# Differential attention with a routed FFN: the sum of the two scaled softmaxes as an accumulating transfer

## The reference

```python
A1 = einsum('bhqd,bhkd->bhqk', Q1, K1) * s        # Q and K have two halves of 64 each
A2 = einsum('bhqd,bhkd->bhqk', Q2, K2) * s
P = softmax(A1) - lam * softmax(A2)
O = einsum('bhqk,bhkd->bhqd', P, V)
Y = concat_heads(O) @ Wo + bo                      # then a layer norm over 128, times 0.2
```

## Time and profile before

| what | us |
|---|---|
| median of 3 runs (1209.81 to 1214.95) | 1213.73 |
| the profiled execution's own time | 1207.97 |
| its span | 1206.2 |
| TensorE busy | 1168.2 (97%) |
| GpSimd busy | 1017.3 (84%) |
| ScalarE busy | 968.9 (80%) |
| VectorE busy | 905.6 (75%) |
| the additions on GpSimd, 256 in all | 609.0 |
| the scalings on GpSimd, 256 in all | 307.1 |

### The profile page before, as it was taken

How to read it: one execution, slowest core, us unless ns; L and a number is a source line. 1 busy time by engine, 2 the same in 40 slices (tenths; PEclk the granted TensorE clock), 3 DMA queues, 4 the chain that set the end, 5 groups by cost and what they waited for, 6 DMA issues and landing times.

```text
span 1206.2 us, 28081 instructions
## 1 busy us (share of the span) xinstructions
PE 1168.2 (97%) x9730; PEld 841.2 (70%) x9730; DVE 905.6 (75%) x1573; ACT 968.9 (80%) x1711; POOL 1017.3 (84%) x657
## 2 busy tenths in 40 slices
PE   5899999999999999999999999999999999998998
PEld 4666767666677776767676767676767776765797
DVE  8878878786787878887878887877887877874510
ACT  3398888887888888988888988888888888985432
POOL 3599999999999999999999999999999999989000
PEclk8999999999999999999999999999999999997999
DMA  8832211221112111222221112221112221110000
GB/s 208 312 80 51 50 44 49 49 49 42 23 39 49 49 49 44 49 49 49 49 49 40 30 34 49 49 49 43 49 49 49 49 49 42 25 28 1 1 18 18
DMA packets 74134, 63.41 MB, mean 53 GB/s; under 512 B 45172, under 2 KB 63092, under 8 KB 74100
## 3 DMA queue, kind: packets, MB, share of 16 engines
q1 hardware_dynamic: 73092, 62.78, 20.3%
q10 hardware_dynamic: 880, 0.19, 0.1%
q0 software_dynamic: 128, 0.01, 0.0%
HBM read 19.96 MB, written 9.44 MB: 24 GB/s over the span
## 4 chain that ended last, share of the span: by engine, by line
PE 75%; POOL 19%; DVE 4%; issue 1%; ACT 0%; DMA 0%; DVEq 0%; SPq 0%; POOLq 0%; ACTq 0%
PE ps L517 24%; PE ps L533 18%; PE ps L547 16%; POOL p_mix L431 11%; PE ps L472 7%; POOL work L428 5%; PE ps L559 4%; PE ps L611 3%; PE ps L598 2%; PE ps L499 1%; DVE pt L862 1%; DVE small L906 1%; POOL wqk_lo L343 1%; POOL w L406 0%; POOL wqk_hi L340 0%
## 5 line engine op out<-in xcount | busy, mean ns | idle before, releaser
L906 DVE TENSOR_REDUCE small<-ps 128x1 f32<-128x1024 f32 x512 | 613.8, 1220 | 114.6 <-PE ps L517 113.9
L431 POOL TENSOR_TENSOR p_mix<-p_mix,work 128x1024 f32<-128x1024 f32 x256 | 609.0, 2379 | 21.4
L533 PEld LDWEIGHTS ps<-ident,p_mix 64*128 64x128 f32 x4096 | 309.6, 139 | 191.7 <-issue 168.1
L725 ACT ACTIVATE pt<-ps 128x512 f32<-128x512 f32 x512 | 305.6, 597 | 131.2 <-PE ps L533 120.7
L533 PE MATMUL ps<-ident,p_mix 64*128 64x64 f32 x4096 | 352.6, 226 | 15.7 <-POOL p_mix L431 11.2
L428 POOL TENSOR_SCALAR work<-work,small 128x1024 f32<-128x1024 f32 x256 | 307.1, 1200 | 42.8 <-DVE small L931 42.8
L712 ACT ACTIVATE p_mix<-ps,small 128x1024 f32<-128x1024 f32 x256 | 284.8, 1113 | 15.4 <-DVE small L906 15.3
L712 ACT ACTIVATE work<-ps,small 128x1024 f32<-128x1024 f32 x256 | 284.4, 1111 | 12.5 <-DVE small L906 12.5
L547 PE MATMUL ps<-pt,v_h 128*64 128x512 f32 x1024 | 248.7, 606 | 0.0
L517 PE MATMUL ps<-k_hi,q_hi 64*128 64x512 f32 x512 | 234.4, 458 | 3.7 <-ACT p_mix L712 1.7
L517 PE MATMUL ps<-k_hi,qx_hi 64*128 64x512 f32 x512 | 230.5, 450 | 0.0
(11 more groups left out here) (135 smaller groups left out, 1305.3 us busy)
## 6 DMA issues: line engine op xcount, KB each, us to landing
qx_hi<-q_hi SPq DMA_DIRECT2D x64, 256.0 KB, 3.7
qx_lo<-q_lo SPq DMA_DIRECT2D x64, 256.0 KB, 4.6
v_scratch<-pt SPq DMA_DIRECT2D x16, 512.0 KB, 3.5
v_h<-v_scratch SPq DMA_DIRECT2D x32, 256.0 KB, 2.9
wqk_raw<-in_L_attn_Wk SPq DMA_DIRECT2D x31, 64.0 KB, 1.7
wqk_raw<-in_L_attn_Wq SPq DMA_DIRECT2D x31, 64.0 KB, 1.9
wo_dup<-in_L_attn_Wo SPq DMA_DIRECT2D x2, 512.0 KB, 7.1
w_raw<-in_L_ffn_W1e SPq DMA_DIRECT2D x4, 256.0 KB, 3.2
```

The costliest lines, as they stand in the source:

```text
L431: pool.tensor_tensor(e1, e1, e2, ALU.add).then_inc(mix_done, 1)
L533: mm = pe.transpose(pt_ps[:, c * D:(c + 1) * D], p_mix[rows, col:col + P], ident[rows, rows])
L725: act.activation(pt4[:, kb % 2, :, j * P + half * D:j * P + (half + 1) * D], pt_ps.rearrange("p (c q) -> p c q", c=KC), ACT.Copy).then_inc ...
L906: dve.tensor_reduce(neg_max[:, m:m + 1], slot[SLOT[k, s]], AX.X, ALU.max, negate=True)\
```

## The change

The addition on GpSimd becomes a transfer that GpSimd issues from e2 to e1 with an add in it (`accum_op`), 128 partitions x 4 KB. Its completion is counted in one semaphore for each of the 4 buffers, by 16. A helper, `mix_landed`, turns a step into the semaphore and the count to wait for, and the two engines that waited for `mix_done` wait with it, for the same steps as before. Nothing else is changed.

```diff
-        scaled, mix_done = sem("scaled"), sem("mix_done")
+        scaled, mixed = sem("scaled"), [sem(f"mixed{i}") for i in range(4)]
...
+        def mix_landed(eng, g, k):
+            if k < 0:
+                g, k = g - 1, k + BODY
+            if not isinstance(g, int) or g >= 0:
+                eng.wait_ge(mixed[k % 4], 16 * (g * (BODY // 4) + k // 4 + 1))
...
                     pool.wait_ge(scaled, n)
-                    pool.tensor_tensor(e1, e1, e2, ALU.add).then_inc(mix_done, 1)
+                    pool.dma_start(e1, e2, accum_op=ALU.add).then_inc(mixed[km % 4], 16)
...
                 if half == 0:
-                    pe.wait_ge(mix_done, n + 1)
+                    mix_landed(pe, g, k - LAG)
...
                 else:
-                    after(act, mix_done, n - 3)
+                    mix_landed(act, g, k - 4)
```

## The result

The changed kernel takes 1360.39 us (median of 4 runs, 1358.23 to 1366.42) against 1211.77 us before in the same comparison: ratio 1.1259, 95% interval 1.1226 to 1.1291. It is 12.6% slower. The forecast was 1289, with 1241 to 1320 as its own range and 1201 to 1450 for 8 in 10. The direction is right and the mechanism is the one named.

The account below looks back on a forecast made before the run. TensorE was taken to bound the middle at 16.42 us per four-step block. Front -7.9, last head -5, stalls +88 give +75 us on 1208.0, so 1283, and 1289 as median; own range 1241 to 1320, 8 in 10 1201 to 1450.

Parts of the forecast that it names:

- The bound and the relief: TensorE sets the middle's pace, 16.42 us a block; removing GpSimd's additions gains nothing there, 13 us elsewhere.
- The front: Six heads that GpSimd bounds, 112.61 to 317.57 us: relief brings 34.16 down to 32.84 us each, 7.9 us gained.
- the first head: Later landing of the first P eats what the faster pace brings: 0, between -2 and +2 us.
- the end: Last head, after 1036 us, where GpSimd is loaded again: relief gains 5 us, between 2 and 9.
- The tight phase: TensorE's turn at j = 2, once in four steps: 3.96 us free, stall 1.4 us a block, +88 us.
- ScalarE's wait on the same semaphores: Before ScalarE overwrites e2 of step n-4: that P has already landed, so no added stall.
- The landing: GpSimd's accumulating transfer, issue to landing: 3.5 + 1.27 + 0.57 = 5.3 us against 3.96 free.
- My base of 3.5: Landing time of a plain store of the same 512 KB, taken as the transfer's floor: 3.5 us.
- 1.27 for the second read: Transfer's extra read of 512 KB at 412 GB/s, the fastest stretch: at least 1.27 us.
- SP's queue only shares the engines: SP's crossing copies, 1 MB a head, 20 us ahead of their use: no cost counted.
- The clock: the rival: TensorE's clock also falls if landing exceeds 5.9 us, 1.7 us lost a block: 1428 to 1510 us; chance 0.20.
- The relief in the changed kernel: GpSimd busy some 550 us instead of 1017; the front's heads no longer than the middle's.

Follow-up runs that it names:

- run 1: Kernel before with the addition left out and no transfer in its place: 1190.86 us, ratio 0.9842.
- run 2: Changed kernel with the add taken out of the transfer, a plain copy of e2 over e1: 1219.45 us, ratio 1.0093.
- Run 5: Changed kernel with SP's crossing copies of Q and loads of V cut to a small part from the third head on: 1299.49 us, ratio 1.0761.
- Run 3: Changed kernel with the reciprocals at j = 0 moved between the two maxima, about 1.0 us earlier: 1355.48 us, ratio 1.1197.
- runs 8 and 10: Changed kernel with additions back on GpSimd except one step in four (n mod 4 = 2), 1348.57 us; or except one a head (n mod 8 = 2), 1341.25 us.
- Run 4: Changed kernel with 8 more matmuls of unread result on TensorE ahead of the tight turn: 1342.75 us, ratio 1.1101.
- run 7: Changed kernel with the additions of n mod 4 = 3 and 0 back on GpSimd, the other two still transfers: 1254.23 us, ratio 1.0372.

## Why the prediction was right, and where its sizes were off

**The bound and the relief: right.** TensorE's 16.42 us a block bounds the middle, and taking the additions away changes nothing there (run 1). The front was worth 8.0 us there against 7.9. The total relief is 18, not 13: the first head was mis-sized (6.4 against 0), the end too (3.2 against 5).

**The tight phase: right.** One wait in four steps, 64 of them, at the turn with j = 2, each block passing it on to the next. ScalarE's wait on the same semaphores cost nothing that the profile shows.

**The landing: right on average, wrong as one number.** I took 5.3 us for issue and landing, against 3.96 free. By the chain it is 0.10 us from the reciprocals to the scaling, 0.29 from the scaling to the issue, 4.55 to land and 0.14 to TensorE: 5.1 us, and 6.0 with the 5.52 of the other block of a head. The stall is 1.14 and 2.10 us, 1.6 on average, against the forecast 1.4. That this comes near is luck. My base of 3.5 was a store with a queue in front of it, where the plain copy lands in 2.9 (run 2), and I added 0.57 for the issue, although a landing is counted from the issue's start and has it in it. Against these two, 1.27 for the second read was too low (1.7 in run 2), and I had nothing for the gaps. The Trainium skill's rule that an add costs its second source read ("Collectives: The Full Stack", Part 3) fits the engines' time, 2.1 times that of the plain copy. The Trainium skill's fit for one transfer ("DMA: Bandwidth & Descriptors", Anatomy of one DMA) plus that read gave 4.4 us as an estimate, near the undisturbed 4.55.

**The step that failed: "SP's queue only shares the engines".** I asked whether SP's copies would be late and put the price for the transfer at nothing. Run 5, without these transfers, is 61 us faster, the clock's part included. SP's copies and its load of V, issued at 642.71 just ahead of the transfer of 643.80, make one tight landing a head longer by a microsecond, that stall passes 2 us, and the clock falls. Run 3 (7.3 us) and runs 8 and 10 (mostly 8.3 to 8.8) show the same at other distances from the crossing copies.

**The clock: the rival was half the truth.** I had set its threshold by one stall of 1.91 us and gave it to landings over 5.9 us, as a case by itself. The stalls of a head are one shorter and one longer than that, so both cases hold at once. Run 5 shows that 1.91 us is no firm border: there the clock fell now and then behind the short stall too. Run 4 prices the clock at 1.5 us a head, some 48 us. In the middle a head's two stalls and its clock, 1.14 + 2.10 + 1.46 = 4.70 us, make up the 4.86 by which it grew. TensorE's 64 waits for transfers add up to 115.8 us against the forecast 88; the clock is the other large part of the loss, and the forecast's sum had nothing for it.

**The relief in the changed kernel: not as forecast.** I had expected the front's heads to be no longer than the middle's. They take 38.43 us where the middle's take 37.70, and up to the second split the kernel is 12 us later than before. How much of the 18 us survives can't be read off, as stall and relief overlap. GpSimd is busy for 643 us, not some 550, since 256 issues take 0.88 us each instead of 0.57.

## What to carry over

When an operation on an engine that is not the bound becomes a transfer, compare latency with free time, phase by phase of the loop's unrolled block: from the row that makes its input ready to the row that needs its output. Then ask what else is in flight at that moment of each block; here 32 transfers, one a head, with the same free time, cost 5 us or 133 us by their place alone. A stall repeated in a TensorE-bound loop can have a second price, the clock; a single stall in the trace of before may already show what it costs, though not from what length on.

## What the runs showed that was unexpected

- A plain 512 KB copy issued by GpSimd lands in 2.9 us, an accumulating one in 4.55 with nothing beside it, 5.5 to 5.7 when issued a microsecond behind the load of V, 6.9 just ahead of the crossing copies (run 7), 7.3 to 8.8 beside or behind them.
- Half the partitions take the whole time, with the other half in flight beside them: 4.4 us at the least for 256 KB, 4.5 for 512 KB.
- Stalls of the same 1.1 to 1.2 us are not all alike: in run 5 most blocks took 17.56 us, a few 18.3 to 19.2, and the run's mean clock was 0.979.
- With one hidden transfer a head the TensorE-bound head grew from 32.84 to 33.02 us, with nothing else on the chain. In the head looked at, the growth lies in the scores behind each projection, 1.42 to 1.43 us instead of 1.34, in both blocks, though only one has a transfer. The cause stays open.
